# A CIN kernel: chunk 5's x is split ahead of A's third round, VectorE sums W1's last tiles, and chunk 5's picks move behind x1's first two tails

## The reference

```python
X0 = inputs.reshape(-1, NUM_FIELDS, EMBED_DIM)
Xi = X0
for W, b in ((W1, b1), (W2, b2), (W3, b3)):
    Wr = W.reshape(out_ch, NUM_FIELDS, m)
    Xi = jnp.einsum('bhd,bmd,ohm->bod', X0, Xi, Wr) + b[None, :, None]
    pools.append(Xi.sum(axis=-1))
concat = jnp.concatenate(pools, axis=-1)
return concat @ fc_W.T + fc_b
```

## Time and profile before

| what | us |
|---|---|
| median of 3 runs | 81.9 (81.87 to 82.09) |
| profiled execution, its own time | 81.76 |
| its span | 80.0 |
| TensorE busy | 72.5 (91%) |
| VectorE busy | 46.6 (58%) |
| ScalarE busy | 34.6 (43%) |
| GpSimd busy | 49.8 (62%) |
| granted TensorE clock, mean share of full speed | 0.998 |

### The profile page before, as it was taken

One profiled execution on the slowest core, in us unless ns is written; L12 is line 12 of the kernel. 1 busy time (PEld: TensorE's weight loads), 2 busy tenths in 40 slices (PEclk: granted clock), 3 DMA queues, 4 the chain that ended last, 5 costly groups with the idle time before them and its releaser, 6 DMA issues.

```text
span 80.0 us, 1146 instructions
## 1 busy us (share of the span) xinstructions
PE 72.5 (91%) x372; PEld 51.6 (65%) x372; DVE 46.6 (58%) x44; ACT 34.6 (43%) x51; POOL 49.8 (62%) x49
## 2 busy tenths in 40 slices
PE   4969499978999669999999999999999999999970
PEld 1315177843445356888888888888888888886840
DVE  1058699686859999289699819992003003213541
ACT  1833997279948956890864700552300300000000
POOL 4989846999994399738079989809955004162400
PEclk9999999999999999999999999999999999999999
DMA  1899999999995615439997000000000000000000
GB/s 22 250 362 266 368 370 351 381 386 390 372 330 163 189 37 135 117 69 381 394 335 307 12 4 0 4 0 0 0 0 0 0 0 0 0 8 0 0 0 0
DMA packets 7529, 12.01 MB, mean 150 GB/s; under 512 B 835, under 2 KB 3971, under 8 KB 7267
## 3 DMA queue, kind: packets, MB, share of 16 engines
q1 hardware_dynamic: 6915, 11.16, 40.8%
q10 hardware_dynamic: 608, 0.77, 3.1%
HBM read 10.88 MB, written 1.05 MB: 149 GB/s over the span
## 4 chain that ended last, share of the span: by engine, by line
PE 77%; DMA 7%; POOL 5%; ACT 3%; DVE 2%; issue 2%; SPq 1%; POOLq 0%; DVEq 0%
PE a_ps L581 28%; PE x_ps L581 25%; DMA w_sb<-w 7%; PE z_ps L575 6%; PE a_ps L674 5%; PE a_ps L636 2%; PE x_ps L609 2%; PE a_ps L635 2%; PE a_ps L647 2%; POOL w_sb L305 2%; POOL z_lo L309 2%; POOL xs L259 2%; DVE r_in L477 2%; PE a_ps L661 1%; PE x_ps L749 1%
## 5 line engine op out<-in xcount | busy, mean ns | idle before, releaser
L266 POOL TENSOR_TENSOR feat<-r_in,feat 128x1024 fp32r<-128x1024 f32 x8 | 19.2, 2403 | 4.6 <-ACT feat L360 4.1
L581 PE MATMUL x_ps<-feat,w_hi 128*128 128x512 f32 x64 | 19.0, 395 | 0.0
L581 PE MATMUL a_ps<-feat,a_hi 128*128 128x512 f32 x64 | 16.2, 395 | 0.0
L259 POOL TENSOR_TENSOR xs<-x_in,xs 32x512 fp32r<-32x512 f32 x7 | 10.8, 1548 | 7.6 <-ACT xs L360 7.3
L504 DVE SCALAR_TENSOR_TENSOR x<-a_ps,vec,x 128x512 f32<-128x512 f32 x7 | 5.2, 746 | 17.7 <-PE a_ps L636 17.7
L273 POOL TENSOR_TENSOR x<-x 128x512 f32<-128x512 f32 x6 | 7.8, 1292 | 10.7 <-DVE x L504 10.5
L581 PEld LDWEIGHTS x_ps<-feat,w_hi 128*128 128x128 f32 x64 | 11.9, 188 | 3.4 <-issue 0.8
L581 PEld LDWEIGHTS a_ps<-feat,a_hi 128*128 128x128 f32 x64 | 11.9, 188 | 2.7
L484 DVE TENSOR_TENSOR feat<-z_ps,feat 128x1024 fp32r<-128x1024 f32 x8 | 9.8, 1220 | 3.5 <-ACT feat L360 3.4
L360 ACT ACTIVATE feat<-z_ps 128x1024 fp32r<-128x1024 f32 x8 | 8.2, 1022 | 5.8 <-DVE z_ps L477 5.8
L581 PE MATMUL x_ps<-feat,w_lo 128*128 128x512 f32 x32 | 9.8, 391 | 0.0
(11 more groups left out here) (76 smaller groups left out, 74.7 us busy)
## 6 DMA issues: line engine op xcount, KB each, us to landing
w_sb<-w SPq DMA_DIRECT2D x9, 512.0 KB, 8.7
x_in<-xl SPq DMA_DIRECT2D x8, 256.0 KB, 7.3
r_in<-xr SPq DMA_DIRECT2D x2, 1024.0 KB, 6.0
a_by_fields<-at_sb SPq DMA_DIRECT2D x8, 96.0 KB, 2.1
x<-x ACTq DMA_DIRECT2D x1, 512.0 KB, 4.5
x<-x SPq DMA_DIRECT2D x1, 512.0 KB, 6.2
w_sb<-w SPq DMA_DIRECT2D x1, 256.0 KB, 11.6
a_by_fields<-at_sb SPq DMA_DIRECT2D x4, 64.0 KB, 2.1
```

What stands on the lines that cost most here:

```text
L259: nc.gpsimd.tensor_tensor(xs[rows, c, :], x_in[rows, c % X_BUFS, :], xs[rows, c, :].bitcast(f32), ALU.subtract).then_inc(xs_lo, 1)
L266: nc.gpsimd.tensor_tensor(feat[:, c, 1, of_half(1), :], z_of(c, 1), feat[:, c, 0, of_half(1), :].bitcast(f32), ALU.subtract).then_inc(lo_d ...
L581: nc.tensor.matmul(bank, weights[:, k, :], feat[:, c, part, k, :], start=(start and k == 0), stop=False)
```

## The change

ScalarE takes `hi(1, 1)` ahead of `split_x(3)`. Behind `hi(3, 0)` it takes the copy of W1's last tiles and `split_x(5)`, which had come behind `hi(3, 1)`, so both now stand ahead of `save_a(2)` and `save_a(3)`. `save_x1(0)` goes between the two halves of `hi(4)`, and `save_zz(1)` ahead of the four read-back DMAs. GpSimd no longer sums W1's last tiles; VectorE does, between its two multiplications of chunk 3. `rest_lo` comes ahead of chunk 4's multiplications, which had come ahead of it. On TensorE `pick_right(5, 0)` and `spread16(1)` change places around x1's tails, and `pick_right(5, 1)` goes into the middle of chunk 2's x1 product.

```diff
--- before.py
+++ after.py
@@ -129,6 +129,7 @@
         zeros_done, fcb_in = sem("zeros_done"), sem("fcb_in")
         fc2_done, b23_done = sem("fc2_done"), sem("b23_done")
         w_sum, w_hi_done, w_lo_done = sem("w_sum"), sem("w_hi_done"), sem("w_lo_done")
+        w_rest_sum = sem("w_rest_sum")
         f_sum, a_hi_done, a_lo_done = sem("f_sum"), sem("a_hi_done"), sem("a_lo_done")
         vt_ready, vt_saved, v_ready, v_saved = sem("vt_ready"), sem("vt_saved"), sem("v_ready"), sem("v_saved")
         q_ready, q_saved, a_ready, a_saved = sem("q_ready"), sem("q_saved"), sem("a_ready"), sem("a_saved")
@@ -323,10 +324,7 @@
             split_x(4)
             pool.wait_ge(xs_lo, 5)
             lo(2)
-            pool.wait_ge(w1_rest_in, 16)
-            nc.gpsimd.tensor_tensor(w1_sb[:, 0, EVEN:, :], w1_sb[:, 0, EVEN:, :], w1_sb[:, 1, EVEN:, :],
-                                    ALU.add).then_inc(w_sum, 1)
-            pool.wait_ge(w_sum, 2)
+            pool.wait_ge(lo_done[1], 3)
             split_x(5)
             pool.wait_ge(xs_lo, 6)
             lo(3)
@@ -398,8 +396,8 @@
             save_zz(0)
             split_x(2)
             hi(1, 0)
+            hi(1, 1)
             split_x(3)
-            hi(1, 1)
             act.wait_ge(vt_ready, 1)
             copy(vt_sb[:, :], vt_ps).then_inc(vt_saved, 1)
             act.wait_ge(v_ready, 1)
@@ -414,24 +412,24 @@
             save_a(0)
             save_a(1)
             hi(3, 0)
+            act.wait_ge(w_rest_sum, 1)
+            copy(w1_hi[:, EVEN:, :], w1_sb[:, 0, EVEN:, :]).then_inc(w_hi_done, 1)
+            split_x(5)
             save_a(2)
             save_a(3)
             hi(3, 1)
-            act.wait_ge(w_sum, 2)
-            copy(w1_hi[:, EVEN:, :], w1_sb[:, 0, EVEN:, :]).then_inc(w_hi_done, 1)
-            split_x(5)
             hi(4, 0)
-            hi(4, 1)
             act.wait_ge(vec_in, 16)
             save_x1(0)
+            hi(4, 1)
             save_x1(1)
+            save_zz(1)
             act.wait_ge(zeros_done, ZEROS)
             act.wait_ge(a_out, A_OUT)
             for j in range(J):
                 k = 1 if j == 0 else 0
                 act.dma_start(f2[H * j:H * j + H, k:TILES, :], bass.AP(
                     scratch.tensor, (TILES * j + k) * M, [[(EXT + 1) * M, H], [1, (TILES - k) * M]])).then_inc(f_main_in, 16)
-            save_zz(1)
             hi(5, 0)
             hi(5, 1)
             act.wait_ge(v_saved, 1)
@@ -498,6 +496,12 @@
                 nc.vector.tensor_tensor(main_hi[rows, EVEN:, :], whole[rows, EVEN:, :],
                                         main_hi[rows, EVEN:, :].bitcast(f32), ALU.subtract).then_inc(done, 1)
 
+            def rest_sum():
+
+                dve.wait_ge(w1_rest_in, 16)
+                nc.vector.tensor_tensor(w1_sb[:, 0, EVEN:, :], w1_sb[:, 0, EVEN:, :], w1_sb[:, 1, EVEN:, :],
+                                        ALU.add).then_inc(w_rest_sum, 1)
+
             def product(c):
                 dve.wait_ge(x1_saved, c + 1)
                 dve.wait_ge(b_ready, c + 1)
@@ -519,12 +523,13 @@
             main_lo(w1_sb[:, 0, :, :], w1_hi, w1_lo, w_lo_done)
             chunk(1)
             chunk(2)
-            chunk(3)
-            mult(4, 0)
-            mult(4, 1)
+            mult(3, 0)
+            rest_sum()
+            mult(3, 1)
+            lo(3)
             dve.wait_ge(w_hi_done, 2)
             rest_lo(w1_sb[:, 0, :, :], w1_hi, w_lo_done)
-            lo(4)
+            chunk(4)
             chunk(5)
             dve.wait_ge(f_main_in, F_MAIN)
             nc.vector.tensor_tensor(f1[:, 0:TILES, :], f1[:, 0:TILES, :], f2[:, 0:TILES, :], ALU.add).then_inc(f_sum, 1)
@@ -710,13 +715,17 @@
             x1_lo(1, 0)
             pick_right(4, 1)
             x1_hi(1, 1)
-            pick_right(5, 0)
             x1_lo(1, 1)
             x1_tail(0)
             x1_tail(1)
+            spread16(1)
+            pick_right(5, 0)
+            x1_hi(2, 0)
+            x1_lo(2, 0)
             pick_right(5, 1)
-            spread16(1)
-            x1_product(2)
+            x1_hi(2, 1)
+            x1_lo(2, 1)
+            x1_tail(2)
             x1_product(3)
             x1_product(4)
             pe.wait_ge(v_saved, 4)
```

## The result

| | us |
|---|---|
| before, median of 4 | 81.89 (81.83 to 82.09) |
| changed, median of 4 | 81.13 (81.09 to 81.42) |
| ratio | 0.9913, 95% interval 0.9898 to 0.9928 |
| changed, profiled execution | 81.42, span 79.6 |

The kernel is 0.76 us faster. The forecast was 81.4 with a range of 81.0 to 82.0: the direction was right, the gain larger than the 0.45 us forecast. All times here are of executions with a mean granted TensorE clock of 0.996 or more: of the version with rest_lo back, two of four executions took 84.5 us at 0.976 and 0.978 and are left out of its time.

What follows compares the result with a forecast made beforehand. TensorE's list bounds the end from 31.9 us; 2.0 us are lost just before. 18 matmuls from 26.96 plus a 0.11 seam end at 31.21, not 31.73: 0.52, less 0.07, gives 0.45 us, so 81.4 us, range 81.0 to 82.0.

Steps and rivals of the forecast that it cites:

- the loss sits between 24.66 and 31.73: TensorE: 22 matmuls there would take 5.06 us in a stream and take 7.07, so 2.0 us are lost.
- the sum on VectorE is held by GpSimd: VectorE's sum of W1's last tiles waits for GpSimd's low part of chunk 2 (24.15), ending 0.28 us later, 24.43.
- rival 2: Slower: W1's last tiles land late and hold VectorE; slower from a landing at 24.47, 82.3 at 25.3; chance 0.09.
- rival 1: VectorE's blocked sum needs its full 0.41 us behind 24.15, ending about 24.65; gain 0.25, 81.6 us; chance 0.19.
- the sign: In the changed kernel's profile, VectorE's new sum ends at 24.4; an end after 24.6 makes the prediction wrong.
- The prediction's estimate from it: VectorE's sum, with about 115 ns for release plus the full 0.41 us, would end at 24.68 instead of 24.43.
- Pick (4, 0) at 25.82, pick (4, 1) at 26.96: TensorE's chunk 4 picks start then, behind VectorE's later multiplication and lo(3): 1.16 and 0.11 us lost.
- The wait for chunk 5's x gone: GpSimd's chunk 5 split ends at 26.86, not 28.57; TensorE's picks (5, 0) and (5, 1) have 0.6 and 1.2 us spare.
- A's chain with 1.5 us to spare: A's read-back starts near 30.05; A's high part is ready at 38.82, TensorE wants it at 40.34: 1.5 us left.
- rival 3: A's high part comes late, ready near 40.0 or 41.2; at the latter 0.4 us slower, 82.3; chance 0.07.
- The sum, 0.45 us: TensorE's stretch ends at 31.21 instead of 31.73, 0.52 us; less 0.07 for a seam, forecast 0.45 us less.
- the charge for a seam: One more seam between kinds of TensorE matmul, up to 0.11 us; 0.07 us taken off the gain.

Runs made afterwards that it cites:

- the version with rest_lo back: The kernel with W1's last-tiles sum back on GpSimd, with rest_lo on VectorE again behind both multiplications of chunk 4: 83.09 us, ratio 1.0138.
- the execution of 81.07 us: The changed kernel measured again without any edit, for one further profile: 81.07 us, span 79.3.
- The version that closes the stretch: The changed kernel with the sum of W1's last tiles back on GpSimd, between its low part of chunk 2 and split of chunk 5: 80.06 us, ratio 0.9776.

## Why the prediction was right

1. **That the loss sits between 24.66 and 31.73 and all gains there arrive at the end.** Right. In the execution of 81.07 us pick (5, 0) and all behind it ran without a wait, but for the 0.4 us at the very end that the kernel before has too. The version that closes the stretch is 1.72 us ahead at x1 of chunk 3 (32.98 against 34.70) and 1.70 us at the end of its profiled execution (80.06 against 81.76).

2. **That the sum on VectorE is held by GpSimd and ends at GpSimd's end plus 0.28 us, whatever the landing.** Right in all profiles, while the landing moved over more than 1 us; rival 2 (the transfer) is out for this range. The full 0.41 us behind the release, rival 1, was not seen either. The landing itself was not at 23.9 as read from the kernel before, but at 22.77 in the first profile and 23.75 in the second. The prediction called itself wrong if the sum ended after 24.6, and it did in two of the six profiles (24.68 and 24.86); in both GpSimd ended later than its 24.15 (24.41 and 24.59), so the sign was set too tight, and the rule held.

   The Trainium skill (SBUF — State Buffer, "A bandwidth-pool intuition that's wrong") gives its about 115 ns for a DMA whose descriptors wait for VectorE's end, which is not this case. The prediction's estimate from it, with the full time on top, is too long here: the sum needs 0.27 to 0.28 us in all behind GpSimd's end for 256 columns.

3. **Pick (4, 0) at 25.82, pick (4, 1) at 26.96.** 25.96 and 27.10 in the first profile, 25.68 and 26.81 in the second: the time was off by 0.14 us either way. Two terms make that up. GpSimd ended at 24.41 and 24.11 instead of 24.15, which moves from execution to execution. And I let the multiplication start 0.03 us behind the sum; it started 0.07 us ahead of its end (24.61 against 24.68, 24.32 against 24.39). That is 0.1 us sooner in both.

4. **The wait for chunk 5's x gone, both picks in time, the tails 1.7 us behind rest_lo.** Right: no wait in the profile, and undoing the picks brings one of 1.32 us, for VectorE. The 0.6 us to spare at pick (5, 0) were 0.37 in the first profile, as multiplication (4, 1) ended at 29.91 and not at 29.5. But the cause was partly misread. I gave the gain to the early split and the later picks together; the runs give the early split nothing in this kernel. The later picks alone give 0.35 us and end at a wait for rest_lo, so what must be added to them is an earlier end of rest_lo. That is argued from this wait: its place ahead of chunk 4 was undone only in the version with the sum on GpSimd, so its own share in the changed kernel stays open.

5. **"save_x1(0) runs from 29.4 behind hi(4, 0); TensorE needs it at 30.8", filed under what costs nothing.** It does cost nothing as changed, but it is a needed part: without the moves of ScalarE 0.86 us come back.

6. **A's chain with 1.5 us to spare.** That it has time to spare was right, and rival 3 did not come. The size was wrong: VectorE's first sum escaped the block, as it started 0.19 us ahead of GpSimd, and A's high part was ready at 36.60 for a product that starts at 40.43, 3.8 us later. The prediction had counted this sum as held.

7. **The sum, 0.45 us.** Too small: measured 0.76 (0.59 to 0.84 by the interval). The time lies in the stated range, but a gain over 0.6 us had been given a chance of only 0.05. That the first profiled execution took 81.42 us, so close to the forecast, is luck: errors nearly cancel there, GpSimd's late end against the hand-off of point 3 and the seam below. Profile against profile, the execution of 81.07 us stands 0.69 us under that of before. Of the 0.24 us missing, 0.1 is the hand-off of point 3, 0.04 GpSimd's earlier end (24.11, not 24.15), and 0.07 the charge for a seam that I took off at the end: pick (5, 1) between x1's matmuls shows none (31.95 to 32.41 is a stream of 0.23 us). The rest, 0.03, is rounding. That the median gain is 0.07 larger than this pair of profiles is within the scatter of both.

## What to carry to other kernels

Before work is moved to another engine, look at what the two engines hold against each other, not only at their busy shares: here a sum of 0.42 us made VectorE's next multiplication 1.2 to 1.7 us later (24.32 to 24.79 instead of 23.09), as it waited first for its transfer and then for GpSimd, and cost the kernel 1.05 us, while GpSimd had room for it. A wait that is taken away shows what the next one is; try each part of a change with and without the others, since of the parts undone here one was worth nothing and one cost time. And where two engines exclude each other, arriving second by 0.03 us can cost an instruction over 1 us: rest_lo took 1.54 us instead of 0.42.

## What was not expected of the hardware

- The block falls on whoever is second and lasts for the other's whole instruction: 32x256 elements on VectorE took 0.42 us alone, 0.97 us, 1.54 and 2.48 us behind GpSimd, each time ending 0.28 to 0.29 us behind GpSimd's end. GpSimd's instruction of 2.40 us took 2.75 us when it came 0.19 us behind VectorE's sum of 0.68 us.
